# Weighing expert results in place, and copying them to the scatter's buffer on ScalarE

## The reference

```python
gating = jax.nn.softmax(X @ Wg + bg, axis=-1)
top_k_indices = jnp.argsort(gating, axis=-1)[..., -TOPK:]
h1 = jnp.einsum('bsd,edh->bseh', X, W1) + b1
h3 = jnp.einsum('bsd,edh->bseh', X, W3) + b3
h = jax.nn.silu(h1 * h3)
expert_outputs = jnp.einsum('bseh,eho->bseo', h, W2) + b2
topk_out = jnp.take_along_axis(expert_outputs, top_k_indices[..., None], axis=2)
topk_w = jnp.take_along_axis(gating, top_k_indices, axis=-1)
mixed = jnp.sum(topk_w[..., None] * topk_out, axis=2)
return mixed @ Wf + bf
```

## Time and profile before

| | |
|---|---|
| median of 3 runs | 1390.75 us (1387.23 to 1391.78) |
| profiled execution | 1396.48 us, its span 1394.8 us |
| mean granted TensorE clock | 0.947 |
| TensorE busy | 1199.2 us, 86% of the span |
| VectorE busy | 955.1 us, 68% |
| ScalarE busy | 772.0 us, 55% |
| GpSimd busy | 605.6 us, 43% |

### The profile page before, as it was taken

The page is one execution under the profiler, slowest core; times in us unless marked ns, Lnnn a source line. Parts: engine busy times, 40 slices in busy tenths (PEclk is TensorE's granted clock), DMA queues, the critical chain, the costliest instruction groups (busy, mean ns, idle before and its releaser), DMA issues. The chain is left out here.

```text
span 1394.8 us, 47057 instructions
## 1 busy us (share of the span) xinstructions
PE 1199.2 (86%) x18189; PEld 883.1 (63%) x18205; DVE 955.1 (68%) x2145; ACT 772.0 (55%) x1344; POOL 605.6 (43%) x651
## 2 busy tenths in 40 slices
PE   4689888889888888888887439999999999999995
PEld 3456555455555455555554228888888888888885
DVE  7245767777777677767775437777677767777775
ACT  1256777777677777767657214444444444444442
POOL 3121142644546445454434633444444445444444
PEclk9889999999999999999998669999999999999998
DMA  5386374665656647564542444566645654644443
GB/s 173 112 212 188 90 199 108 181 171 133 199 148 185 150 131 206 145 188 122 155 134 71 154 138 55 71 127 123 121 55 72 139 104 66 127 66 65 63 67 46
DMA packets 210988, 176.48 MB, mean 127 GB/s; under 512 B 115451, under 2 KB 175483, under 8 KB 210827
## 3 DMA queue, kind: packets, MB, share of 16 engines
q1 hardware_dynamic: 153482, 116.86, 33.5%
q0 software_dynamic: 25728, 34.17, 13.8%
q10 hardware_dynamic: 31616, 23.19, 6.1%
HBM read 66.95 MB, written 89.89 MB: 112 GB/s over the span
## 5 line engine op out<-in xcount | busy, mean ns | idle before, releaser
L1027 DVE TENSOR_REDUCE mx<-p_max 128x4 f32<-128x496 f32 (+1 forms) x248 | 213.1, 859 | 144.0 <-PE p_max L1295 140.8
L1574 PE MATMUL p_h<-xt_parts,w_hi 128*128 128x256 f16 x1824 | 276.0, 274 | 11.2 <-DVE xt_parts L1660 11.1
L837 ACT ACTIVATE probs<-p_exp,unscale 128x736 f32<-128x736 f32 (+1 forms) x256 | 210.4, 822 | 94.4 <-PE p_exp L1295 81.9
L1722 POOL DMA_INDIRECT out<-yw,tokens x136 | 218.2, 1605 | 42.9 <-POOL tick L1721 28.2
L1574 PEld LDWEIGHTS p_h<-xt_parts,w_hi 128*128 128x128 f16 x1824 | 177.7, 98 | 36.9 <-DVE t L1664 11.9
L1664 DVE SCALAR_TENSOR_TENSOR t<-p_h,b,t 128x256 f32<-128x256 f32 x272 | 126.3, 480 | 106.5 <-ACT t L1613 104.9
L1721 POOL TENSOR_TENSOR tick<-tick 128x1 f32<-128x1 f32 x136 | 69.6, 512 | 275.9 <-DVE yw L1687 275.9
L1613 ACT ACTIVATE t<-p_h,b,undo 128x256 f32<-128x256 f32 x272 | 142.2, 558 | 79.4 <-PE p_h L1574 70.6
L1574 PE MATMUL p_h<-xt_parts,w_lo 128*128 128x256 f16 x912 | 175.2, 274 | 0.0
L706 POOL TENSOR_TENSOR qk_lo<-qf,qk_hi 128x512 f16<-128x512 f32 x64 | 76.5, 1200 | 172.5 <-ACT qk_hi L821 172.5
L1618 ACT ACTIVATE hf<-t 128x512 f32<-128x512 f32 x136 | 85.7, 630 | 110.2 <-DVE t L1664 110.2
(11 more groups left out here) (272 smaller groups left out, 2494.3 us busy)
## 6 DMA issues: line engine op xcount, KB each, us to landing
qk_dram<-qk_hi SPq DMA_DIRECT2D x128, 128.0 KB
qs<-qk_dram SPq DMA_DIRECT2D x64, 192.0 KB, 4.2
ks<-qk_dram SPq DMA_DIRECT2D x64, 192.0 KB, 4.4
x_in<-in_x SPq DMA_DIRECT2D x64, 128.0 KB, 2.4
qk_dram<-qk_lo SPq DMA_DIRECT2D x64, 128.0 KB
w_mat<-in_W ACTq DMA_DIRECT2D x32, 256.0 KB
out<-x_sb SPq DMA_DIRECT2D x64, 128.0 KB
w_split<-w_first_hi SPq DMA_DIRECT2D x24, 256.0 KB
```

What stands on the lines that cost most here:

```text
L837: nc.scalar.activation(probs[r % 3][:, :, 0:hi - lo].rearrange("p (e s) w -> p e s w", e=2), p_exp[:, :, 0:2 * WIN].rearrange("p e (s w) - ...
L1027: nc.vector.tensor_reduce(out=maxes, in_=max_buffer(r, p_max, p_exp)[:, :, 0:2 * WIN].rearrange("p e (s w) -> p e s w", s=2)[:, :, :, 0:hi ...
L1574: last = nc.tensor.matmul(p_h[:, m % KC, k, :], w[e][a][:, k, HID * c + P * m:HID * c + P * m + P], xt[:, x, c, :], start=(n == 0 and c == ...
L1722: nc.gpsimd.indirect_dma_start(out=io["out"].rearrange("b s d -> (b s) d"), out_offset=bass.IndirectOffsetOnAxis(ap=tokens[:, b, :].bitcas ...
```

## The change

VectorE's `weigh` now writes the product back into `y`, without waiting for a scatter, and increments `s_yg`. It moves from behind the second `split` to right behind `take_result`. ScalarE's `take_tokens` becomes `send`: for each block it waits for `s_yg` and for the scatter, copies the tokens, and copies `y` to `yw`, which increments `s_yw`. GpSimd waits for `s_yw` alone; `s_tok` is gone. `take_result` waits for `s_yw` as before, which ScalarE now increments.

```diff
--- before.py
+++ after.py
@@ -1506,7 +1506,7 @@
         s_fill, s_rows, s_words, s_tc = sem("s_fill"), sem("s_rows"), sem("s_words"), sem("s_tc")
         s_h, s_t1, s_p, s_silu, s_lo = (sem(n) for n in ("s_h13", "s_t1", "s_prod", "s_silu", "s_hlo"))
         s_r, s_y, s_yw, s_tick = sem("s_result"), sem("s_y"), sem("s_yw"), sem("s_tick")
-        s_tok = sem("s_tok")
+        s_yg = sem("s_y_weighed")
         s_sc = [sem(f"s_ysc{b}") for b in range(NB)]
         block = ctx.enter_context(nc.Block())
         MAX_TILES = TOKENS // FT
@@ -1618,15 +1618,16 @@
                 nc.scalar.activation(hf[q][:], t3[q][:], ACT.Silu).then_inc(s_silu, 1)
 
             def load_words(at, g):
-                after(act, s_tok, NB * g)
                 after(act, s_yw, NB * g)
                 act.dma_start(words[:], io["routed"][bass.ds(at, FT), 2 * D:2 * D + USED].rearrange("(b p) r -> p b r", p=P)).then_inc(s_words, 16)
 
-            def take_tokens(g):
+            def send(g):
                 act.wait_ge(s_words, 16 * g + 16)
                 for b in range(NB):
+                    act.wait_ge(s_yg, NB * g + b + 1)
                     after(act, s_sc[b], 16 * g)
-                    nc.scalar.activation(tokens[:, b, :], words[:, b, M_TOKEN:M_TOKEN + 2], ACT.Copy).then_inc(s_tok, 1)
+                    nc.scalar.activation(tokens[:, b, :], words[:, b, M_TOKEN:M_TOKEN + 2], ACT.Copy)
+                    nc.scalar.activation(yw[:, b, :], y[:, b, :], ACT.Copy).then_inc(s_yw, 1)
 
             def body(e, p, before, at):
                 g = 0 if p is None else p + 1
@@ -1639,7 +1640,7 @@
                 first_factor(e, g, 3)
                 silu(g, 1)
                 if p is not None:
-                    take_tokens(p)
+                    send(p)
 
             at = None
             for e in range(NE):
@@ -1650,7 +1651,7 @@
                 at = e * REGION + count * FT - FT
             last_tile = load_last(act, NE - 1)
             load_words(at, last_tile)
-            take_tokens(last_tile)
+            send(last_tile)
 
         @block.vector
         def _(dve):
@@ -1683,9 +1684,8 @@
                 dve.drain()
                 dve.wait_ge(s_words, 16 * g + 16)
                 for b in range(NB):
-                    after(dve, s_sc[b], 16 * g)
-                    nc.vector.scalar_tensor_tensor(yw[:, b, :], y[:, b, :], words[:, b, M_GATES + 2 * e:M_GATES + 2 * e + 2].bitcast(F32),
-                                                   kept["bf_half"][:], ALU.mult, ALU.add).then_inc(s_yw, 1)
+                    nc.vector.scalar_tensor_tensor(y[:, b, :], y[:, b, :], words[:, b, M_GATES + 2 * e:M_GATES + 2 * e + 2].bitcast(F32),
+                                                   kept["bf_half"][:], ALU.mult, ALU.add).then_inc(s_yg, 1)
 
             def body(e, p, before):
                 g = 0 if p is None else p + 1
@@ -1697,9 +1697,8 @@
                 split(e, g, p, 0)
                 if p is not None:
                     take_result(before, p)
+                    weigh(before, p)
                 split(e, g, p, 1)
-                if p is not None:
-                    weigh(before, p)
 
             copy_columns(0)
             last_tile = tiles(dve, body)
@@ -1716,7 +1715,6 @@
                 for b in range(NB):
                     if p is not None:
                         pool.wait_ge(s_tick, NB * p + b + 1)
-                    pool.wait_ge(s_tok, NB * g + b + 1)
                     pool.wait_ge(s_yw, NB * g + b + 1)
                     nc.gpsimd.tensor_tensor(tick[:, b:b + 1], tick[:, NB:NB + 1], tick[:, NB:NB + 1], ALU.add).then_inc(s_tick, 1)
                     nc.gpsimd.indirect_dma_start(out=io["out"].rearrange("b s d -> (b s) d"), out_offset=bass.IndirectOffsetOnAxis(
```

## The result

The changed kernel takes **1382.7 us** (median of 20 runs, 1375.74 to 1387.85) against 1390.74 us of the kernel before (20 runs, 1385.04 to 1395.05): ratio 0.9938, 95% interval 0.9922 to 0.9953. The profiled execution took 1385.31 us (span 1383.6).

The account below looks back on a forecast made before the run. TensorE was taken to bound the kernel at 7.86 us a tile over 68 tiles. Terms 0 + 0.8 - 0.7 = +0.1 us on the profiled 1396.48 us; with the median 5.7 us lower, 1391 us, range 1384 to 1401.

Parts of the forecast that it names:

- The likeliest case, no change: Whole kernel: time stays the same, own range 1387 to 1395 us, chance 0.57.
- Steady tiles 0 us: Tiles away from stalls: the next first factor starts where it does now, TensorE keeps 7.86 us a tile, 0 us.
- The copy, 0.41 us: ScalarE's added copy of 128x256 from SBUF, two a tile: 0.41 us each, bounds 0.20 and 0.56.
- ScalarE's ring 7.36 us, under TensorE's 7.86: ScalarE from one tile's first factor to the next, behind a stall: 7.36 us, or 7.66 with copies of 0.56.
- VectorE's ring: VectorE from one tile's product through split and weighing to the next: 7.44 us, instructions as before.
- The slower rival: ScalarE's tokens and copies before the first factor become the bound: 1401 us at 8.0 a tile, 1414 at 8.20; chance 0.23.
- The rings behind a stall: Where TensorE holds nobody up, ScalarE needs 7.36 us a tile and VectorE 7.44, both under TensorE's 7.86.
- A scatter that starts 0.67 us earlier is worth 0: Late scatters behind weight loads land no earlier for earlier issue: 0 us, bounds +0.07 and -0.67 in each of five stalls.
- The faster rival: Scatters land as much earlier as they start, stalls shrink and both half-clock stretches go: 1384.4 us, chance 0.20.
- Late words +0.8: Three waits for words: VectorE waits and weighs before ScalarE copies, so the first factor is 0.27 us later each, +0.8 us.
- The tail -0.7: Last tile's wait for the scatter of the one before: issued 0.7 us earlier, it lands that much earlier, -0.7 us.
- The tick held by `h_lo`: GpSimd's tick beside VectorE's split: if held until `h_lo` ends, scatters start no earlier, tail gain gone, 1391.6 us.

Follow-up runs that it names:

- The doses: Changed kernel with a GpSimd addition of 128x256, 128x352 or 128x640 ahead of each tile's first tick: 1383.05, 1384.64 and 1403.17 us.
- The held-back scatters: Changed kernel with a GpSimd addition of 128x256 (0.63 us) ahead of each tile's first tick: 1383.05 us, ratio 0.994.
- Two runs: Changed kernel with a GpSimd addition of 128x256 or 128x352 ahead of each tile's first tick: 1383.05 us (0.994) and 1384.64 us (0.9962).
- the dose of 128x640: Changed kernel with a GpSimd addition of 128x640 ahead of each tile's first tick: 1403.17 us, ratio 1.0087.
- the dose of 0.8 us: Changed kernel with a GpSimd addition of 128x352 (0.79 us) ahead of each tile's first tick: 1384.64 us, ratio 0.9962.

## Why the prediction was wrong

The likeliest case, no change, was wrong. Its mechanism for steady tiles held and its reading of what follows a stall did not.

- *Steady tiles 0 us*: right. 7.86 us a tile, again full.
- *The copy, 0.41 us*: 0.400. The Trainium skill's formula (ScalarE: Activation LUTs, What ACT_TABLE_LOAD costs) gave 0.40 as an estimate; the trace agrees.
- *ScalarE's ring 7.36 us, under TensorE's 7.86*: right in that it does not bind. Behind a stall `y` follows `y` at 1132.68 and 1140.04, 7.36 us, and the copies are 7.31 us apart at best. The doses, which drew out VectorE's `h_lo` by 0.19, 0.35 and 0.83 us, raised this to 7.50, 7.66 and 8.14, each by its full length: so it is VectorE's ring (7.44 forecast), and ScalarE's is no longer. The slower rival did not come; with the weighing behind the split it did (8.72 us).
- *The rings behind a stall*: **this step failed**. The prediction added up ScalarE's ring (7.36 us) and VectorE's own (7.44 us) and no other. They were not wrong (copies 7.31 to 7.37 us apart), but they were not what bound the kernel before. Behind most of its stalls the bound was the loop over two tiles through the second scatter, 15.70 us, which I could have added up from the trace. I read the 144.9 us of waits for scatters in a steady tile, where TensorE sets the pace and the wait is slack, and not behind a stall, where the same wait closes a loop.
- *A scatter that starts 0.67 us earlier is worth 0*: **this term failed**, and it is where the 8 us are; its own bound, 0.67 us in each of five stalls, was under half of them. The new order shortens the loop by the 0.67 us and by 0.6 to 1.0 us of landing (3.8 to 4.2 us behind a stall for 4.8), since the scatter no longer meets the columns' load so closely. The held-back scatters speak for the landing as the larger part: without the earlier start the gain stayed. Behind weight loads landings moved about as much as their issue: the second scatter was issued 4.1 us and landed 10.5 us after the first weights DMA in the mean of six experts before, 3.3 and 9.5 us now (9.2 to 10.0). Words and first scatter landing together, which I took for the drain of the load, held in five of six experts before and within 0.4 us in four of six now; in the other two the words were there 2.5 and 2.9 us ahead.
- *The faster rival* (1384.4 us) had the right signs, fewer and shorter stalls and no stretch at half clock (the 3.7 us came as priced), but for 0.67 us a stall, not for a lead that is regained between experts; that its 1384.4 us lie near the measured 1382.7 is in part luck. Measured: stalls -6.4 us, for -2.8 forecast there.
- *Late words +0.8*: too small to see; ScalarE's wait for words is now VectorE's, 7.4 us in 4 for 9.9 in 3.
- *The tail -0.7*: -1.7 between the two executions. The last scatter of a tile is issued at 1373.45 and tokens follow at 1377.30, 3.85 us, as in the earlier trace rows.
- *The tick held by `h_lo`*: did not happen, and was not put to the test: the tick took 0.21 us, ran beside `h_hi` and was over before `h_lo` began. The rule (the Trainium skill, SBUF — State Buffer, Who interferes with whom) shows in the doses instead, where a 128x256 to 128x640 addition on GpSimd drew `h_lo` out to 0.94, 1.10 and 1.58 us.

What stays open: why, behind weight loads, the second scatter of the kernel before lands 0.8 to 1.9 us after the first and in the changed one 0.8 to 1.5; how the transposing load holds up a scatter; why at like distances (1.0 to 1.1, or 1.75 us) landings differ between kernels; and how the 8 us divide. Two runs gave the earlier start back and kept 8 and 5 us, so most is not the start in itself, but both also kept the new order on VectorE; the one run that moved the columns' load alone gained 4.1 us net of its cost at the experts' starts. The profiles are single executions, and runs of one kernel spread over some 10 us.

## What to carry to other kernels

Where a buffer's reuse waits for a transfer, add up the loop through that wait (landing, next use, next issue, landing) behind a stall, not in the steady state: a loop that is no shorter than what the bounding engine needs for the tiles it spans makes no stall good, and the stalls then add up, though each wait in a steady tile looks like slack. And look what other transfer starts within a microsecond of one that is waited for.

## What the runs showed of the hardware

- An indirect scatter-add of 128 rows landed 3.8 us (median) behind its start with no such load near. In the kernel before it took 4.2 to 4.4 us with a transposing DMA of 256 rows 1.0 us behind it, and 4.6 to 5.4 with one 0.8 us behind it; in the changed kernel with the dose of 128x640 4.0 (median) with one 1.05 us behind it.
- Stalls of 2.48 and 2.65 us were followed by a stretch at 0.50 of the clock, one of 1.43 by none; with the dose of 0.8 us a stall of 2.2 had none either. The length alone does not decide: a stall of 2.15 us (changed kernel, columns 0.8 us later) was followed by one, a stall of 2.71 us (kernel before, columns 2.7 us later) by none.
- VectorE's `h_lo` (two inputs from SBUF) beside a GpSimd addition of 1.27 us that began 0.23 us ahead of it took 1.58 us instead of 0.75. Beside additions of 0.63, 0.79 and 1.27 us, of which 0.40, 0.56 and 1.04 us were left when it began, it took 0.19, 0.35 and 0.83 us longer: each time the rest less 0.21 us.
